# The last tile's rounding, transposes and bank copy shared between two engines, in an attention and ternary feed-forward kernel

## The chip, the cores and the metric

The kernel runs on one core of a Trainium2 chip. The metric is the device time of one execution in microseconds (us). The kernel before has a median of 99.2 us over 3 runs (99.07 to 100.43).

## The reference

`x` has 16 sequences of 56 tokens with 256 features (896 tokens in all). The layer is cross attention and then a feed-forward with ternary weights and activations quantised per token. Cut to what matters here:

```python
x = x + xattn(layernorm(x), ctx, Wq, Wkv_expand, Wout)       # 16 heads of 16, causal
def quant_weight(w): s = mean(|w|) + 1e-5; return clip(round(w / s), -1, 1), s
def quant_act(x):    s = max(|x|, axis=-1) / 127 + 1e-5; return clip(round(x / s), -128, 127), s
def qlinear(x, w):   return einsum(quantised x, quantised w) * xs * ws
h = silu(qlinear(y, w_gate)) * qlinear(y, w_up)               # y = layernorm(x); h: 896 x 1024
x = x + qlinear(h, w_down)                                    # 896 x 256
```

The change lies in the last step, for the last 128 tokens: `h` is multiplied by 1/s of its token, rounded, transposed and multiplied by `w_down`.

## The kernel before

The 896 tokens are 7 tiles of 128. Each engine has an instruction stream of its own, written as loops over slots `s`; semaphores order the engines. Slots 0 to 7 hold attention, slots 8 to 17 the feed-forward. Tile `t` is in gate and up products at slot `t + 8` (`GU0`), in the transposes of the gated values at slot `t + 10` (`HT0`), in the down product at slot `t + 11` (`DN0`). For the last tile, t = 6, these are slots 14, 16 and 17.

For one tile the tail of the feed-forward is this. VectorE (DVE) writes `h_sb` in two halves of 512 columns (L808), takes the row maxima (L815), the scale (L822), its reciprocal `r_tok` (L829) and `s_out` (L831). `round_h` (L302) then writes the rounded codes of a half into `h_int`, an alias of `wf_sb`, which is the name that the profile shows. `ROUNDER` gives the engine of each half: GpSimd (POOL) for tiles 0 to 5, DVE for both halves of tile 6. TensorE (PE) transposes eight 128x128 blocks as f16 into one PSUM bank (`transpose_gated`, L1100), ScalarE (ACT) copies the whole bank to `hT` (`read_misc`, kind `ht`, L552 in its helper), and PE multiplies the eight blocks of `hT` with `wdT` into a bank (`down_projection`, through the helper of L892). The end of a tile is `FINISHER`: tiles 0 to 4 are scaled by ACT (L620) and added to `x` by POOL (L519); tiles 5 and 6 are finished by one DVE instruction (`add_down_product`, L847). Both write `o_sb`, which the profile calls `k_wide`. SP waits for the tiles in order and issues one output DMA of 128 KB each (L394).

The four PSUM banks `bank0` to `bank3` are shared by all jobs: `misc_no` numbers the jobs, a job takes bank `n % 4`, and `take_bank` makes PE wait until the reader of job `n - 4` is done. At the end the order of jobs is `ht` 4, `dn` 3, `ht` 5, `dn` 4, `ht` 6, `dn` 5, `dn` 6. The order on the engines there is:

- PE: slot 16 is transposes of tile 6, then the down product of tile 5; slot 17 is the down product of tile 6.
- POOL: in a slot first the roundings of tile `s - 8`, then `add_residual` of tile `s - 11`. Slot 14 holds tile 6's roundings (none before) and the add of tile 3; slot 15 the add of tile 4.
- DVE: slot 14 holds tile 6's roundings; slot 16 the finish of tile 5, slot 17 the finish of tile 6.

Of the kernel before, what the change touches and what calls it, by code (L numbers as in the profile page):

```python
# [5 lines left out]
ALU = mybir.AluOpType  # L6
# [3 lines left out]
P = 128  # L10
# [9 lines left out]
HT0 = GU0 + 2  # L20
# [42 lines left out]
             (3, 'gpsimd'): [(1, 0, 1), (1, 1, 1)]}  # L63

ROUNDER = [('gpsimd', 'gpsimd'), ('gpsimd', 'gpsimd'), ('gpsimd', 'gpsimd'), ('gpsimd', 'gpsimd'), ('gpsimd', 'gpsimd'),
           ('gpsimd', 'gpsimd'), ('vector', 'vector')]

FINISHER = ['gpsimd', 'gpsimd', 'gpsimd', 'gpsimd', 'gpsimd', 'vector', 'vector']

# [1 line left out]
def xattn_ffn(nc, x, ctx_512, wq, wkv, wout, w_gate, w_up, w_down, out):  # L71
# [47 lines left out]
    for t in range(NT):  # L119
        misc[XQ_SLOTS[t]] += [("xqT", t)]  # L120

    misc_no = {job: n for n, job in enumerate(misc[-1])}
    for s in range(SLOTS):
        at_jobs = [("aT", s - 2)] if 0 <= s - 2 < NP - 1 else []
        tr_jobs = [("tr", s - 1, 0), ("tr", s - 1, 1)] if 0 <= s - 1 < NP else []
        op_jobs = [("op", OP_AT[s])] if s in OP_AT else []
        pv_jobs = [("pv", s - 1)] if 0 <= s - 1 < NP else []
        ht_jobs = [("ht", s - HT0)] if 0 <= s - HT0 < NT else []
        dn_jobs = [("dn", s - DN0)] if 0 <= s - DN0 < NT else []
        at_last = [("aT", NP - 1)] if s == NP else []  # L130
        for job in at_jobs + tr_jobs + misc[s] + op_jobs + pv_jobs + at_last + ht_jobs + dn_jobs:
            misc_no[job] = len(misc_no)
# [4 lines left out]
    with ExitStack() as ctx:  # L137
# [158 lines left out]
        def round_h(eng, ops, engine, t, c):  # L296
            if ROUNDER[t][c] != engine:
                return
            eng.wait_ge(r_ready, t + 1)
            if t >= 2:  # L300
                eng.wait_ge(misc_written, misc_no[("ht", t - 2)] + 1)
            ops.tensor_scalar(h_int[:, t % 2, c, :], h_sb[:, t % 3, GC * c:GC * c + GC], r_tok[:, 1, t:t + 1], CODED,  # L302
                              ALU.mult, ALU.add).then_inc(hint_ready[engine, c], 1)

# [27 lines left out]
        def read_misc(eng, copy, job):  # L332
            n = misc_no[job]
            kind, i = job[0], job[1]
            bank = MI[n % NB]
            eng.wait_ge(misc_written, n + 1)
            if kind == "wkvT":
                last = copy(wkvT[:, :], bank[:, :])
            elif kind == "ctxT":
                last = copy(ctxT[:, 0:KT], bank[:, 0:KT])  # L340
            elif kind == "k":
                (j0, j1), hfs = job[2:]
                width = 2 * S * (j1 - j0)
                last = copy(kT[:, i, hfs[0]:hfs[-1] + 1, 2 * S * j0:2 * S * j1],
                            bank[:, 0:len(hfs) * width].rearrange("p (i k) -> p i k", i=len(hfs)))
            elif kind in ("wqT", "woT"):
                last = copy((wqT if kind == "wqT" else woT)[:, :, :],
                            bank[:, :].rearrange("p (i o) -> p i o", i=HALVES))
            elif kind == "xT":
                last = copy(xnT[:, :, P * i:P * i + P], bank[:, 0:C].rearrange("p (i o) -> p i o", i=HALVES))  # L350
            elif kind == "q":
                p0, p1 = job[1:]
                last = copy(qT[:, :, 2 * p0:2 * p1, 0:S],
                            bank[:, 0:2 * CT * (p1 - p0) // 2].rearrange("p (i b q) -> p i b q", i=HALVES, q=S), scale=SCALE)
            elif kind == "v":
                eng.wait_ge(pads_ready, 1)
                for par in range(2):
                    last = copy(v_wide[:, VB * i:VB * i + VB, :, HV * par:HV * par + HD],
                                bank[:, :].rearrange("p (b h d) -> p b h d", b=VB, d=HD),
                                scale=parity_mask[:, par:par + 1])  # L360
            elif kind == "mean":
                last = copy(w_scale[:, i:i + 1], bank[:, 0:1], bias=EPS)
            elif kind == "tr":

                if i >= 2:
                    eng.wait_ge(misc_written, misc_no[("pv", i - 2)] + 1)
                n0 = 4 * 2 * S * job[2]
                last = copy(pT[:, i % 2, n0:n0 + 4 * 2 * S].rearrange("p (m b q) -> p m b q", m=4, b=2),
                            bank[:, :].rearrange("p (m b q) -> p m b q", m=4, b=2)[:, :, :, 0:S])
            elif kind == "aT":  # L370
                last = copy(attnT[:, :, 2 * S * i:2 * S * i + 2 * S].rearrange("p i (b q) -> p i b q", b=2),
                            bank[:, 0:C].rearrange("p (i b q) -> p i b q", i=HALVES, b=2)[:, :, :, 0:S])
            elif kind == "xqT":
                codes = bank[:, :].bitcast(F16)[:, 0:C].rearrange("p (i o) -> p i o", i=HALVES)
                last = copy(xqT[:, i, :, :], codes, scale=256.0, bias=-1536.0)
            elif kind == "ht":
                if i >= 2:
                    eng.wait_ge(misc_written, misc_no[("dn", i - 2)] + 1)
                last = copy(hT[:, i % 2, :, :], bank[:, :].bitcast(F16).rearrange("p (c q) -> p c q", c=NC8),
                            scale=256.0, bias=-1536.0)  # L380
            last.then_inc(misc_read[n % NB], 1)

        @block.sync
# [156 lines left out]
        def _(act):  # L540
# [68 lines left out]

            def read_gated(s):  # L610
                if 0 <= s - HT0 < NT:
                    read_misc(act, copy, ("ht", s - HT0))

            def scale_down_product(s):
                t = s - DN0
# [29 lines left out]
        def _(dve):  # L645
            def copy(dst, src, scale=None, bias=None):
                if bias is not None:
                    return nc.vector.tensor_scalar(dst, src, 1.0, bias, ALU.mult, ALU.add)
                if scale is not None:
                    return nc.vector.tensor_scalar(dst, src, scale, 1.0, ALU.mult, ALU.mult)  # L650
                return nc.vector.tensor_copy(dst, src)  # L651
# [182 lines left out]
            def round_gated(s, c):  # L834
                t = s - GU0
                if 0 <= t < NT:
                    round_h(dve, nc.vector, "vector", t, c)

            def add_down_product(s):
                t = s - DN0  # L840
                if 0 <= t < NT:
                    if FINISHER[t] != "vector":
                        return
                    n = misc_no[("dn", t)]
                    dve.wait_ge(misc_written, n + 1)
                    dve.wait_ge(dn_scale_ready, t + 1)
                    nc.vector.scalar_tensor_tensor(o_sb[:, t, :], MI[n % NB][:, 0:C], s_out[:, 2, t:t + 1],  # L847
                                                   x_sb[:, t, :], ALU.mult, ALU.add).then_inc(misc_read[n % NB], 1)
# [18 lines left out]
            for s in range(NT_SLOT0, SLOTS):  # L867
                if s == NT_SLOT0:
                    divide_by_sums(s - 2)
                token_maxima(s)  # L870
                add_attention(s)
                token_scales(s)
                second_stats(s)
                gate_up_scales(s)
                invert_token_scales(s)
                second_moments(s)
                read_misc_banks(s, 0, None)
                if s == NT_SLOT0:
                    divide_by_sums(s - 1)
                gate_times_up(s, 0)  # L880
                gate_times_up(s, 1)
                gated_maxima(s)
                gated_scales(s)
                invert_gated_scales(s)
                round_gated(s, 0)
                round_gated(s, 1)
                add_down_product(s)

        @block.tensor
        def _(pe):  # L890
# [200 lines left out]
            def transpose_gated(s):  # L1091
                t = s - HT0
                if 0 <= t < NT:
                    codes_out = take_bank(("ht", t))[:, :].bitcast(F16)
                    for h in range(NG):
                        pe.wait_ge(*rounded(t, h))
                        codes = h_int[:, t % 2, h, :].bitcast(F16)
                        for c in range(HC):
                            c0 = GC * h + P * c
                            last = nc.tensor.transpose(codes_out[:, c0:c0 + P], codes[:, 2 * P * c:2 * P * c + 2 * P:2],  # L1100
                                                       ident_h[:, :])
                    last.then_inc(misc_written, 1)

            def down_projection(s):
                t = s - DN0
                if 0 <= t < NT:
                    bank = take_bank(("dn", t))
                    if t == 0:
                        pe.wait_ge(wt_in[2], 16)
                    wait_read(pe, ("ht", t))  # L1110
                    for c in range(NC8):
                        last = mm(bank[:, 0:C], hT[:, t % 2, c, :], wdT[:, :, c, :],
                                  start=(c == 0), stop=(c == NC8 - 1))
                    last.then_inc(misc_written, 1)
# [45 lines left out]
```

## Time and profile before

| | us |
|---|---|
| median of 3 runs | 99.2 |
| lowest and highest | 99.07, 100.43 |
| the profiled execution: its time | 99.2 |
| the profiled execution: span of its instructions | 97.4 |
| PE busy in the span | 81.4 (84%) |
| DVE busy | 72.8 (75%) |
| ACT busy | 59.1 (61%) |
| POOL busy | 56.0 (58%) |

The span is the time from the first to the last event on the core; 1.8 us of the execution lie outside it. Starts in rows are in us from the start of the span. The busy shares are averages over stages of different nature, so what a change in one stage brings is read from the rows of that stage.

### The profile page before, as it was taken

What the parts mean: (1) busy time and instruction counts of PE and PEld (TensorE: products, weight loads), DVE (VectorE), ACT (ScalarE), POOL (GpSimd) and SP (SyncE); (2) the same over time, 40 slices, a digit from 0 to 9 for tenths busy, and PEclk for the clock granted to TensorE, in tenths of its full rate; (3) what the DMA queues carried; (4) which work ended last, traced back from release to release, by engine and by line L of the source; (5) the groups of instructions that cost most, each with busy time, mean ns of one, the idle gap of its engine ahead of it and who ended that gap; (6) DMA issues with size and microseconds to landing.
All of it is one profiled execution on the core that took longest, in us unless ns stands there. A gap on an engine that the chain in (4) does not pass through costs nothing.

```text
span 97.4 us, 2408 instructions
## 1 busy us (share of the span) xinstructions
PE 81.4 (84%) x872; PEld 56.7 (58%) x872; DVE 72.8 (75%) x180; ACT 59.1 (61%) x98; POOL 56.0 (58%) x108
## 2 busy tenths in 40 slices
PE   4997779769899859999999988799854989998470
PEld 1345556448559649786978756766322637756250
DVE  4662529789958991699948999375999999999721
ACT  0741413845097973759799799926728478987340
POOL 5650557199507999696948852525286174669400
PEclk9999999999999999999999999999999999999999
DMA  1999999000000000000293908100000000101322
GB/s 32 289 271 357 347 360 365 19 0 0 0 0 7 3 3 7 0 0 0 49 106 71 222 0 187 29 0 0 7 0 0 0 0 3 54 0 61 108 77 84
DMA packets 12579, 7.59 MB, mean 78 GB/s; under 512 B 7960, under 2 KB 12312, under 8 KB 12568
## 3 DMA queue, kind: packets, MB, share of 16 engines
q1 hardware_dynamic: 11292, 6.93, 26.3%
q10 hardware_dynamic: 1276, 0.51, 2.1%
q8 instruction: 7, 0.11, 0.5%
q14 instruction: 4, 0.03, 0.1%
HBM read 4.95 MB, written 0.92 MB: 60 GB/s over the span
## 4 chain that ended last, share of the span: by engine, by line
DVE 43%; PE 35%; issue 8%; DMA 5%; ACT 3%; ACTq 2%; POOL 1%; DVEq 0%; POOLq 0%
PE bank L892 20%; DVE amax L815 9%; DVE h_sb L808 7%; PE sc L892 6%; DMA ctx_sb<-in_ctx_dram 5%; DVE probs L719 4%; PE bank L1021 4%; DVE v_wide L650 3%; PE bank L1045 2%; DVE asum L703 2%; DVE mx L710 2%; DVE xnT L651 2%; DVE attn L734 2%; DVE s_tok L822 1%; DVE x_sb L750 1%
## 5 line engine op out<-in xcount | busy, mean ns | idle before, releaser
L289 POOL TENSOR_TENSOR k_wide<-kT,head_mask 128x896 f32<-128x896 f32 (+1 forms) x9 | 13.1, 1478 | 9.6 <-ACT kT L552 9.6
L892 PE MATMUL sc<-wT,xqT 128*128 128x512 bf16 x56 | 13.9, 380 | 3.4 <-DVE h_sb L808 3.4
L607 ACT ACTIVATE wf_sb<-sc,s_out 128x512 f32<-128x512 f32 x14 | 9.6, 688 | 7.5 <-PE sc L892 5.1
L302 POOL TENSOR_SCALAR wf_sb<-h_sb,r_tok 128x512 f32<-128x512 f32 x12 | 8.2, 692 | 9.5 <-DVE r_tok L829 9.5
L710 DVE TENSOR_REDUCE mx<-sc 128x16 f32<-128x896 f32 x8 | 8.7, 1088 | 3.6 <-PE sc L892 3.4
L808 DVE SCALAR_TENSOR_TENSOR h_sb<-sc,s_out,wf_sb 128x512 f32<-128x512 f32 x14 | 9.9, 740 | 1.1 <-ACT wf_sb L607 1.1
L892 PEld LDWEIGHTS sc<-wT,xqT 128*128 128x128 bf16 x56 | 5.0, 98 | 9.2 <-DVE h_sb L808 5.1
L562 ACT ACTIVATE probs<-probs 128x896 f32<-128x896 f32 x8 | 7.6, 952 | 4.2 <-DVE probs L719 3.8
L892 PEld LDWEIGHTS bank<-v_wide,pT 128*64 128x64 f32 x256 | 8.1, 138 | 2.3 <-issue 2.3
L892 PE MATMUL bank<-xnT,wqT 128*128 128x224 f32 (+1 forms) x40 | 7.4, 329 | 2.1 <-DVE xnT L651 1.5
L892 PE MATMUL bank<-v_wide,pT 128*64 128x34 f32 x256 | 9.0, 226 | 0.0
L552 ACT ACTIVATE hT<-bank 128x1024 bf16<-128x1024 f16 x7 | 7.2, 1023 | 3.0 <-PE bank L1100 2.3
L815 DVE TENSOR_REDUCE amax<-h_sb 128x1 f32<-128x1024 f32 x7 | 8.5, 1220 | 0.2
L719 DVE TENSOR_TENSOR probs<-sc,mx 128x896 f32<-128x896 f32 x8 | 8.7, 1083 | 0.1
L552 ACT ACTIVATE pT<-bank 128x448 f32<-128x448 f32 x16 | 7.8, 542 | 1.4 <-PE bank L1021 1.0
L1021 PE MATMUL bank<-ident,probs 128*128 128x128 f32 x64 | 8.4, 273 | 0.0
L892 PE MATMUL bank<-woT,attnT 128*128 128x256 f32 x28 | 7.6, 394 | 0.4 <-ACT attnT L552 0.4
L892 PEld LDWEIGHTS bank<-xnT,wqT 128*128 128x128 f32 x40 | 6.2, 190 | 2.9 <-issue 2.9
L892 PE MATMUL bank<-wdT,hT 128*128 128x256 bf16 x56 | 7.3, 272 | 0.3 <-ACT hT L552 0.3
L892 PE MATMUL sc<-k_wide,qT 64*64 64x224 f32 x128 | 7.4, 349 | 0.0
L1021 PEld LDWEIGHTS bank<-ident,probs 128*128 128x128 f32 x64 | 7.2, 141 | 0.3 <-ACT probs L562 0.3
L892 PE MATMUL sc<-tern 128*128 128x512 bf16 x14 | 5.8, 574 | 1.3 <-DVE tern L654 1.3
(107 smaller groups left out, 166.9 us busy)
## 6 DMA issues: line engine op xcount, KB each, us to landing
wf_sb<-in_L_ffn_w_gate_dram SPq DMA_DIRECT2D x1, 1024.0 KB, 8.6
wf_sb<-in_L_ffn_w_up_dram SPq DMA_DIRECT2D x1, 1024.0 KB, 11.0
wf_sb<-in_L_ffn_w_down_dram SPq DMA_DIRECT2D x1, 1024.0 KB, 12.3
out_dram<-k_wide SPq DMA_DIRECT2D x7, 128.0 KB, 1.7
x_sb<-in_x_dram SPq DMA_DIRECT2D x2, 256.0 KB, 4.4
x_sb<-in_x_dram SPq DMA_DIRECT2D x1, 384.0 KB, 6.1
wq_sb<-in_L_xattn_Wq_dram ACTq DMA_DIRECT2D x1, 256.0 KB, 4.6
wo_sb<-in_L_xattn_Wout_dram SPq DMA_DIRECT2D x1, 256.0 KB, 8.9
```

The costliest lines, as they stand in the source:

```text
L289: ops.tensor_tensor(k_wide[:, c, hf, :, cols], kT[:, c, hf, None, cols].to_broadcast([P, RH, n]), head_mask[:, 0:RH, None].to_broadcast([P ...
L302: ops.tensor_scalar(h_int[:, t % 2, c, :], h_sb[:, t % 3, GC * c:GC * c + GC], r_tok[:, 1, t:t + 1], CODED, ALU.mult, ALU.add).then_inc(hi ...
L552: return nc.scalar.activation(dst, src, ACT.Copy, scale=scale, bias=bias)
L562: nc.scalar.activation(probs[:, u % R, :, 0:S], probs[:, u % R, :, 0:S], ACT.Exp).then_inc(exp_ready, 1)
L607: nc.scalar.activation(g_sb[:, t % 2, GC * c:GC * c + GC], SC[:, j % 4, :], ACT.Silu, scale=s_out[:, 0, t:t + 1]).then_inc(silu_ready, 1)
L650: return nc.vector.tensor_scalar(dst, src, scale, 1.0, ALU.mult, ALU.mult)
L710: nc.vector.tensor_reduce(mx[:, u % R, :].rearrange("p (r h) -> p r h", r=2), scores_of(u), axis=AX_X, op=ALU.max).then_inc(max_ready, 1)
L719: nc.vector.tensor_tensor(probs[:, u % R, :, 0:S].rearrange("p (r h) k -> p r h k", r=2), scores_of(u), mx[:, u % R, :].rearrange("p (r h) ...
L808: nc.vector.scalar_tensor_tensor(h_sb[:, t % 3, cols], SC[:, j % 4, :], s_out[:, 1, t:t + 1], g_sb[:, t % 2, cols], ALU.mult, ALU.mult).th ...
L815: nc.vector.tensor_reduce(amax[:, 1, t:t + 1], h_sb[:, t % 3, :], axis=AX_X, op=ALU.max, apply_absolute_value=True).then_inc(h_amax_ready, 1)
L892: return nc.tensor.matmul(*a, **k)
L1021: last = nc.tensor.transpose(bank[:, P * m:P * m + P], probs[:, u % R, h0:h0 + 2, :].rearrange("p h k -> p (h k)"), ident[:, :])
```

## The change

The second half of tile 6 is rounded by POOL in place of DVE. The job `("ht", 6)` becomes two jobs `("ht", 6, 0)` and `("ht", 6, 1)` with a bank each; the transposes of each half raise `misc_written` on their own. ACT copies the first bank (512 columns), DVE the second (`read_last_gated`, placed ahead of `add_down_product` in DVE's slot). The down product of tile 6 waits for the first copy before its first block and for the second before its fifth. Tiles 0 to 5 are computed as before, with a job name of three fields. The diff without two lines that only rename:

```diff
-           ('gpsimd', 'gpsimd'), ('vector', 'vector')]
+           ('gpsimd', 'gpsimd'), ('vector', 'gpsimd')]
+    def ht_halves(t):
+        return [("ht", t, 0), ("ht", t, 1)] if t == NT - 1 else [("ht", t, None)]
-        ht_jobs = [("ht", s - HT0)] if 0 <= s - HT0 < NT else []
+        ht_jobs = ht_halves(s - HT0) if 0 <= s - HT0 < NT else []
...
             elif kind == "ht":
                 if i >= 2:
                     eng.wait_ge(misc_written, misc_no[("dn", i - 2)] + 1)
-                last = copy(hT[:, i % 2, :, :], bank[:, :].bitcast(F16).rearrange("p (c q) -> p c q", c=NC8),
-                            scale=256.0, bias=-1536.0)
+                c0, c1 = (0, NC8) if job[2] is None else (HC * job[2], HC * job[2] + HC)
+                codes = bank[:, :].bitcast(F16)[:, 0:P * (c1 - c0)]
+                last = copy(hT[:, i % 2, c0:c1, :], codes.rearrange("p (c q) -> p c q", q=P), scale=256.0, bias=-1536.0)
...
-                    read_misc(act, copy, ("ht", s - HT0))
+                    read_misc(act, copy, ht_halves(s - HT0)[0])
...
-                    return nc.vector.tensor_scalar(dst, src, 1.0, bias, ALU.mult, ALU.add)
+                    return nc.vector.tensor_scalar(dst, src, 1.0 if scale is None else scale, bias, ALU.mult, ALU.add)
...
+            def read_last_gated(s):
+                if s - HT0 == NT - 1:
+                    read_misc(dve, copy, ("ht", NT - 1, 1))
...
                 round_gated(s, 1)
+                read_last_gated(s)
                 add_down_product(s)
...
-                    codes_out = take_bank(("ht", t))[:, :].bitcast(F16)
+                    jobs = ht_halves(t)
                     for h in range(NG):
+                        if h < len(jobs):
+                            codes_out = take_bank(jobs[h])[:, :].bitcast(F16)
                         pe.wait_ge(*rounded(t, h))
                         codes = h_int[:, t % 2, h, :].bitcast(F16)
                         for c in range(HC):
-                            c0 = GC * h + P * c
+                            c0 = P * c + (GC * h if len(jobs) == 1 else 0)
                             last = nc.tensor.transpose(codes_out[:, c0:c0 + P], codes[:, 2 * P * c:2 * P * c + 2 * P:2],
                                                        ident_h[:, :])
-                    last.then_inc(misc_written, 1)
+                        if h >= NG - len(jobs):
+                            last.then_inc(misc_written, 1)
...
-                    wait_read(pe, ("ht", t))
                     for c in range(NC8):
+                        if c % HC == 0 and c // HC < len(ht_halves(t)):
+                            wait_read(pe, ht_halves(t)[c // HC])
                         last = mm(bank[:, 0:C], hT[:, t % 2, c, :], wdT[:, :, c, :],
                                   start=(c == 0), stop=(c == NC8 - 1))
```

## Rows read from the trace of the kernel before

**Rows 1.** Chain of waits, its last part: start us, us, what

```profile
92.11 0.41 PE bank L1100 x4
92.54 1.03 ACT hT L552
93.71 1.05 PE bank L892 x8
94.78 0.48 DVE k_wide L847
```

**Rows 2.** Timeline: start us, us, engine line op out<-in xcount [idle before <-releaser]

```profile
90.48 0.16 DVE L829 RECIPROCAL r_tok<-s_tok 128x1 f32<-128x1 f32 x1
90.68 0.49 DVE L302 TENSOR_SCALAR wf_sb<-h_sb,r_tok 128x512 f32<-128x512 f32 x1
91.04 0.72 POOL L519 TENSOR_TENSOR k_wide<-k_wide,x_sb 128x256 f32<-128x256 f32 x1 [0.58 <-ACT k_wide L620]
...
91.08 0.97 DVE L302 TENSOR_SCALAR wf_sb<-h_sb,r_tok 128x512 f32<-128x512 f32 x1
```

**Rows 3.** Timeline of PE's weight loads, DVE and ACT behind the roundings

```profile
91.28 0.24 PEld L1100 LDWEIGHTS bank<-ident_h,wf_sb 128*128 128x128 f16 x4 [1.15 <-issue]
...
92.10 0.23 PEld L1100 LDWEIGHTS bank<-ident_h,wf_sb 128*128 128x128 f16 x4 [0.58 <-DVE wf_sb L302]
...
92.29 0.81 PEld L892 LDWEIGHTS bank<-wdT,hT 128*128 128x128 bf16 x8
...
93.42 0.48 DVE L847 SCALAR_TENSOR_TENSOR k_wide<-bank,s_out,x_sb 128x256 f32<-128x256 f32 x1 [1.37 <-PE bank L892]
93.68 0.78 PEld L892 LDWEIGHTS bank<-wdT,hT 128*128 128x128 bf16 x8 [0.58 <-issue]
```

**Rows 4.** Timeline of DVE and POOL where they multiply by the head mask

```profile
10.58 0.62 DVE L289 TENSOR_TENSOR k_wide<-kT,head_mask 128x448 f32<-128x448 f32 x1 [1.33 <-ACT kT L552]
10.62 1.38 POOL L289 TENSOR_TENSOR k_wide<-kT,head_mask 128x448 f32<-128x448 f32 x1 [4.17 <-ACT kT L552]
...
16.16 0.93 POOL L289 TENSOR_TENSOR k_wide<-kT,head_mask 128x448 f32<-128x448 f32 x1
```

**Rows 5.** Timeline of tile 5's reciprocal and its roundings on POOL

```profile
87.46 0.16 DVE L829 RECIPROCAL r_tok<-s_tok 128x1 f32<-128x1 f32 x1
...
87.72 0.69 POOL L302 TENSOR_SCALAR wf_sb<-h_sb,r_tok 128x512 f32<-128x512 f32 x1 [0.96 <-DVE r_tok L829]
...
89.05 1.41 POOL L519 TENSOR_TENSOR k_wide<-k_wide,x_sb 128x256 f32<-128x256 f32 x2
```

**Rows 6.** Groups of instructions by line: forms xcount | busy us, mean ns

```profile
L552 ACT ACTIVATE hT<-bank 128x1024 bf16<-128x1024 f16 x7 | 7.2, 1023 | 3.0 <-PE bank L1100 2.3
...
L650 DVE TENSOR_SCALAR v_wide<-bank,parity_mask 128x512 f32<-128x512 f32 x4 | 2.8, 745 | 0.4 <-PE bank L892 0.4
...
L552 ACT ACTIVATE wkvT<-bank 128x512 f32<-128x512 f32 x1 | 0.6, 597 | 1.3 <-PE bank L929 1.3
```

**Rows 7.** Timeline of SP: two early loads, the outputs of tiles 2 and 3, 3, and 6

```profile
2.24 0.92 SPq L311 DMA_DIRECT2D x_sb<-in_x_dram  x2
...
89.80 1.34 SPq L394 DMA_DIRECT2D out_dram<-k_wide  x2
...
90.48 0.66 SPq L394 DMA_DIRECT2D out_dram<-k_wide  x1
...
95.29 0.33 SPq L394 DMA_DIRECT2D out_dram<-k_wide  x1
```

**Rows 8.** Stretches: A:B us, PE, PEld, DVE, ACT, POOL busy (x), PEclk, DMA share, GB/s

```profile
90.70:90.90 0.20, 0.00 (x0) 0.00 (x0) 0.20 (x2) 0.20 (x1) 0.00 (x0) 1.00 0.98 317
...
91.70:91.90 0.20, 0.00 (x0) 0.00 (x0) 0.20 (x1) 0.00 (x0) 0.07 (x1) 1.00 1.03 353
...
96.10:96.30 0.20, 0.00 (x0) 0.00 (x0) 0.00 (x0) 0.00 (x0) 0.00 (x0) 1.00 0.77 266
```

**Rows 9.** DMA issues: KB each, median us from issue to landing

```profile
out_dram<-k_wide SPq DMA_DIRECT2D x7, 128.0 KB, 1.7
```

More of the change, by code:

```diff
@@ L300, in round_h @@
             if t >= 2:
-                eng.wait_ge(misc_written, misc_no[("ht", t - 2)] + 1)
+                eng.wait_ge(misc_written, misc_no[("ht", t - 2, None)] + 1)
             ops.tensor_scalar(h_int[:, t % 2, c, :], h_sb[:, t % 3, GC * c:GC * c + GC], r_tok[:, 1, t:t + 1], CODED,
```

## The prediction

> **What bounds the kernel now.** I read the chain of waits first, and only its end, since everything the change touches lies behind the last tile's scale. The chain ends as DVE rounding, four transposes on PE, the ACT copy of the bank, the eight matmuls of the down product, DVE's finish [rows 1]. Then come the issue of the last output DMA at 95.29, its landing after about 1.7 us, and the last 0.4 us to the end of the span at 97.4 [rows 7, 9]. So the path is serial, and a saving in it moves the end by as much, unless the output DMAs get in the way.
>
> The timeline then says how long each piece is. DVE rounds the two halves one after the other: the first from 90.68 to 91.17, the second from 91.08 to 92.05 [rows 2]. The same instruction on the same shape takes 0.49 the first time and 0.97 the second. Between them POOL began its add of tile 4, at 91.04, 0.04 before DVE's second rounding, and it ended at 91.76 [rows 2]. DVE's end at 92.05 is 0.29 behind POOL's end. My reading is that the two instructions cannot run together and that the later one stood still for 0.97 - 0.49 = 0.48 us. The trace has a second such pair with the roles exchanged: DVE's multiply by the head mask starts at 10.58, POOL's at 10.62; DVE takes 0.62 and POOL 1.38, where the same form takes POOL 0.93 alone [rows 4]. Again the one that began 0.04 later paid, 0.45 us, and it ended 12.00 - 11.20 = 0.80 us behind the other's end, which is 0.13 less than a whole instruction.
>
> Last, the PE rows. Weight loads show the pace of PE's stream best. Behind the second half's transposes the down product of tile 5 starts 0.19 later (92.10 to 92.29) and its eight loads end at 93.10. Tile 6's down product starts loading at 93.68 [rows 3]. The 0.58 us between is the wait for the ACT copy, 92.54 to 93.56 [rows 1], plus 0.12 from its end to PE's load. These two, the second rounding and this gap, are all that the change can shorten.
>
> **The change part by part.** *Rounding.* DVE's first half stays where it is, 90.68 to 91.17. POOL's half waits for the same `r_tok`. In tile 5 POOL's rounding started 0.26 after the start of `r_tok` (87.46 to 87.72) [rows 5]; from 90.48 this gives 90.74, and 0.69 alone would end it at 91.43. But DVE starts 0.06 earlier, and by the two pairs the later one waits. With the 0.13 of start-up that POOL had done in its pair, it ends 0.69 - 0.13 = 0.56 behind 91.17, at 91.73. Against 92.05 that is 0.32 us earlier. The bounds are 91.43 (no conflict, 0.62 earlier) and 91.86 (its whole 0.69 behind DVE's end at 91.17, 0.19 earlier). I take 91.73, as the only pair in which POOL lost shows it.
>
> The Trainium skill has the rule: SBUF — State Buffer, section "SBUF: two separate sides", says that DVE and GpSimd share a port pair that goes whole to the instruction that starts first, while the other blocks. The two pairs here agree, in both orders [rows 2, 4]. Perfetto Trace Analysis, section "Optimizing Scalar/DVE Operations", warns that moving work between these two engines might therefore not help; the full form of that warning, both roundings strictly in series, is the 91.86 above, so by it the saving would be 0.13 smaller. What the warning leaves out is that the series already exists before the change, with a longer add in the middle.
>
> *POOL's queue.* POOL's rounding now stands in slot 14 ahead of the add of tile 3 (queued at 89.05 with tile 2's, two adds in 1.41 [rows 5]) and of tile 4 (91.04). POOL waits with both behind it until 90.74. The adds then run at about 0.70 each: tile 3 to 92.43, tile 4 to 93.13. Who waits for them is SP alone, for the output DMAs. They no longer lie in front of any rounding.
>
> *Transposes and down product of tile 5.* PE's second group waits for POOL: 91.73 plus 0.06 (92.05 to 92.10 before) is 91.79. The down product of tile 5 loads from 91.79 + 0.19 = 91.98, and its loads end at 92.79. The bank numbers move by one: the four last jobs now take the banks of `ht` 4, `dn` 3, `ht` 5 and `dn` 4. The last of their readers is ACT's scaling of `dn` 4, and it ended before POOL could start tile 4's add at 91.04 [rows 2], so PE waits for no bank.
>
> *The copy.* ACT's half takes 0.60 in place of 1.02: the 512-column row, against the 1024-column one [rows 6]. The copy began 0.44 behind the start of the transposes before it (92.10 to 92.54) [rows 1, 3]. The first half's start at 91.28, so ACT copies from 91.72 to 92.32. DVE's half has no row of its own kind (f16 in PSUM to bf16). The nearest is the f32 copy with a scale, 0.745 for 512 columns [rows 6]; the lower bound is 0.49, its quick rounding of as many columns [rows 2]. I take the slow one: it starts at 91.79 + 0.44 = 92.23 and ends at 92.98. PE needs ACT's half at 92.79 and has it 0.47 earlier. It needs DVE's half for the fifth block at 92.79 + 0.40 = 93.19, and 92.98 plus 0.05 to 0.12 is in time by about 0.1. So the gap of 0.58 closes entirely, and its cover is thin for DVE's half only: a copy of 0.95 would cost 0.1 to 0.2.
>
> *DVE's queue.* The copy stands ahead of tile 5's finish. That finish waits for PE until 93.42 - 0.31 = 93.11 [rows 3], so the copy ending at 92.98 delays nothing.
>
> *Sum.* Tile 6's down product loads from 92.79 in place of 93.68: 0.31 by the rounding and 0.58 by the gap, 0.89 together. DVE's finish starts at 94.78 - 0.89 = 93.89, the DMA issue moves from 95.29 to 94.40. Span 97.4 - 0.9 = 96.5; the profiled execution took 99.2, the same as the median, so 99.2 - 0.9 = 98.3 us.
>
> *The output DMAs.* Tile 3's was issued at 90.48 and tile 6's at 95.29, 0.03 behind DVE's finish (94.78 + 0.48) [rows 1, 7]. Now the four come at 92.46, 93.16, 93.62 (93.11 + 0.48 + 0.03) and 94.40, four in 1.94 us in place of 4.81. An issue takes 0.33, but tile 3's, 0.68 behind tile 2's, took 0.66 [rows 7]. At the 266 to 353 GB/s of the transfers' stretches 128 KB need 0.4 to 0.5 us [rows 8], less than the distances between the issues (0.46 to 0.78). Against a slow issue stand the early loads, two issues in 0.92 us [rows 7]. I cost this at nothing and keep 0.3 as an upper bound for a late last transfer.
>
> **The rivals.** *R1, the outputs queue up, and the end comes later than before.* Full data rate came at 90.7 for tile 2 and at 91.7 for tile 3, 1.0 apart, although the issues were 0.68 apart [rows 8]. If 1.0 us is the least distance of two such transfers, tile 3's starts at 92.46 + 0.9 = 93.36 and tile 6's at 96.36, against about 96.15 before [rows 8]: 0.2 later, 99.4 us. It decides from a distance of 0.93 us on. Against it: two early loads were issued in 0.92 together [rows 7], and the one pair shows an excess of only 0.3.
>
> *R2, part of that.* Each close issue costs 0.33 more, and the last one inherits 0.3: 98.6 us.
>
> *R3, POOL comes first.* If POOL's rounding starts before DVE's, DVE ends at 91.43 + 0.29 = 91.72 and POOL at 91.43. PE transposes both halves from 91.77 in one go, and tile 5's down product loads from 92.20 and tile 6's from 93.01: 0.67 gained, 98.5 us. For it: a lead of only 0.06. Against it: POOL's start behind `r_tok` was 0.26, DVE's is 0.20 [rows 2, 5].
>
> *R4, no conflict.* Both roundings free, 91.43: tile 5's down product from 91.72, tile 6's from 92.53, 1.15 gained, 98.05 us. Against it stand both pairs [rows 2, 4].
>
> *R5, no change that shows.* PE waits in the middle of the accumulation for DVE's copy or for the queue of semaphores, or the execution's start moves: 98.9 to 99.3. Only the gap's 0.58 or less would be at stake, as the roundings alone give 0.3.
>
> **How the numbers follow.** The forecast of 98.3 (with the bound of 91.86, 98.4) has 0.55, R1 0.07, R2 0.13, R3 0.08, R4 0.09, R5 0.08. The likeliest case's own range is 98.1 to 98.5. From 97.9 to 98.9 lie the forecast, R2, R3 and R4, 0.85 in all; since other runs of the kernel before spread from 99.07 up I set 97.9 to 99.0. Faster or slower by over 2% (2.0 us, about what a measurement of this kernel tells from no change) needs a time below 97.2 or above 101.2. No case reaches either; I leave 0.03 and 0.02.
>
> **What would show it.** In the profile after: one DVE rounding of about 0.49 at 90.7 and one POOL rounding that takes about 1.0 in place of 0.69 (R4: 0.69; R3: DVE's takes 1.0). The two down products' loads back to back, no idle before the last eight. ACT's last copy 0.60, DVE's 0.5 to 0.75. POOL's two adds behind 91.7. The last DMA issued at about 94.4 with 1.7 us to landing (R1: over 3; R2: about 2.1). It would be wrong if the conflict costs more than one instruction, if the fifth matmul waits, or if the last output waits behind the others.

## The result, and the profile after

The changed kernel has a median of 98.45 us over 9 runs beside 99.2 us of the kernel before. The ratio to the kernel before is 0.9931 (95% interval 0.9902 to 0.9959). Two more comparisons gave 0.9922 (0.9894 to 0.9951) and 0.9946 (0.9917 to 0.9974). In the three comparisons it is faster by 0.5 to 0.8%, some 0.5 to 0.8 us: each interval lies below 1, though the difference is under 2%. The prediction was 98.3 us, 97.9 to 99.0.

Some executions, of the kernel before too, are granted half of TensorE's clock for a stretch in the first 30 us and end 2 to 9 us later: the medians here are over all executions and the ratios over the others alone, the time of a single execution with such a stretch is not compared, and in every profile used below the clock is full in the last 15 us, where the change lies. The start of the last tile's reciprocal also varies by itself, from 90.07 to 91.16 us between the profiles whose span is under 98 us. So I measure the **tail**: from the start of the last reciprocal (`r_tok`) to the start of DVE's last finish (`k_wide<-bank,s_out,x_sb`). It agrees to 0.01 us between the three profiles of the changed kernel (3.55, 3.55, 3.56) and between the two of the version in which ACT rounds (3.23, 3.23); the other versions have one profile each.

The end of the chain of waits in a profile of the changed kernel (the one with the span of 96.4 us); start us, us, what:

```profile
90.22 0.17 DVE r_tok L834
90.40 0.09 issue
90.49 0.99 POOL wf_sb L306
91.48 0.14 issue
91.61 0.38 PE bank L1112 x4
92.00 1.76 PE bank L902 x16
93.76 0.03 issue
93.78 0.48 DVE k_wide L856
```

The ACT copy of [rows 1] is gone from the chain, and the last sixteen matmuls are one piece. The tail is 93.78 - 90.22 = 3.56 us; before it is 94.78 - 90.48 = 4.30 [rows 1, 2]. That is 0.74 less. The same kernel's timeline shows the pieces; they answer [rows 2, 3, 5]:

```profile
90.42 0.49 DVE L306 TENSOR_SCALAR wf_sb<-h_sb,r_tok 128x512 f32<-128x512 f32 x1
90.49 0.98 POOL L306 TENSOR_SCALAR wf_sb<-h_sb,r_tok 128x512 f32<-128x512 f32 x1 [0.96 <-DVE r_tok L834]
91.03 0.24 PEld L1112 LDWEIGHTS bank<-ident_h,wf_sb 128*128 128x128 f16 x4 [1.15 <-issue]
...
91.48 0.60 ACT L557 ACTIVATE hT<-bank 128x512 bf16<-128x512 f16 x1 [0.77 <-PE bank L1112]
91.58 0.24 PEld L1112 LDWEIGHTS bank<-ident_h,wf_sb 128*128 128x128 f16 x4 [0.32 <-issue]
...
91.78 1.68 PEld L902 LDWEIGHTS bank<-wdT,hT 128*128 128x128 bf16 x16
91.83 1.91 PE L902 MATMUL bank<-wdT,hT 128*128 128x256 bf16 x16
...
92.03 0.43 DVE L653 TENSOR_SCALAR hT<-bank 128x512 bf16<-128x512 f16 x1 [1.12 <-PE bank L1112]
...
92.91 0.48 DVE L856 SCALAR_TENSOR_TENSOR k_wide<-bank,s_out,x_sb 128x256 f32<-128x256 f32 x1 [0.45 <-PE bank L902]
93.78 0.48 DVE L856 SCALAR_TENSOR_TENSOR k_wide<-bank,s_out,x_sb 128x256 f32<-128x256 f32 x1 [0.39 <-PE bank L902]
```

POOL's rounding takes 0.98 in place of its usual 0.69, and ends 0.56 behind DVE's. Sixteen weight loads run in one row of 1.68 with no idle before the last eight, where there were 0.58 us [rows 3]. From the end of the last finish (94.26) to the end of the span it is 2.1 us, as before (95.26 to 97.4).

The output DMAs did not pile up. The stretches of the same profile (columns as in [rows 8]) show one transfer's full rate at 93.1, 93.7, 94.3 and 95.1, and the four issues before them took 0.33 each (the last four rows: start us, us, issue on SP):

```profile
93.10:93.30 0.20, 0.20 (x4) 0.18 (x3) 0.20 (x1) 0.00 (x0) 0.00 (x0) 1.00 1.03 353
...
93.70:93.90 0.20, 0.04 (x1) 0.00 (x0) 0.12 (x1) 0.00 (x0) 0.00 (x0) 1.00 0.91 312
...
94.30:94.50 0.20, 0.00 (x0) 0.00 (x0) 0.00 (x0) 0.00 (x0) 0.00 (x0) 1.00 0.98 338
...
95.10:95.30 0.20, 0.00 (x0) 0.00 (x0) 0.00 (x0) 0.00 (x0) 0.00 (x0) 1.00 0.73 251
...
92.19 0.33 SPq L399 DMA_DIRECT2D out_dram<-k_wide  x1
...
92.87 0.33 SPq L399 DMA_DIRECT2D out_dram<-k_wide  x1
...
93.42 0.33 SPq L399 DMA_DIRECT2D out_dram<-k_wide  x1
...
94.30 0.33 SPq L399 DMA_DIRECT2D out_dram<-k_wide  x1
```

### The profile page after: what moved, and what is told of

Read it like the earlier page. It is cut to its first block, busy times and chain, and to the rows that moved or that the text cites. A ratio compares the mean times of both kernels' runs of the same rounds, so it can differ in the third digit from the quotient of the medians.

```text
span 99.1 us, 2411 instructions
## 1 busy us (share of the span) xinstructions
PE 81.9 (83%) x872; PEld 57.4 (58%) x872; DVE 72.4 (73%) x180; ACT 58.6 (59%) x98; POOL 56.9 (57%) x109
## 4 chain that ended last, share of the span: by engine, by line
DVE 41%; PE 37%; issue 7%; DMA 6%; POOL 2%; ACTq 2%; ACT 1%; POOLq 0%; DVEq 0%
PE bank L902 21%; DVE amax L820 9%; DVE h_sb L813 7%; PE sc L902 7%; DMA ctx_sb<-in_ctx_dram 6%; DVE probs L724 4%; PE bank L1031 4%; DVE v_wide L655 3%; PE bank L1055 2%; DVE asum L708 2%; DVE mx L715 2%; DVE xnT L656 2%; DVE attn L739 2%; DVE s_tok L827 1%; DVE x_sb L755 1%
## 5 line engine op out<-in xcount | busy, mean ns | idle before, releaser
L306 POOL TENSOR_SCALAR wf_sb<-h_sb,r_tok 128x512 f32<-128x512 f32 x13 | 9.1, 714 | 10.5 <-DVE r_tok L834 10.5
L557 ACT ACTIVATE hT<-bank 128x1024 bf16<-128x1024 f16 (+1 forms) x7 | 6.7, 962 | 2.2 <-PE bank L1112 1.4
```

The lines of the kernel that those rows point to most:

```text
L557: return nc.scalar.activation(dst, src, ACT.Copy, scale=scale, bias=bias)
```

## The experiments

**The change once more.** The kernel as changed.

> The changed kernel as it is. The tail is read from the start of the last tile's reciprocal (L834 here) to the start of DVE's last finish: 4.30 us in the kernel before (90.48 to 94.78), 3.55 in the changed kernel's first profile. My theory (0.3 from the rounding, 0.6 from the closed gap, a few hundredths lost to PE): 3.5 to 3.6 again, and a median 0.7 to 0.9 us under the kernel before. The rival that the output DMAs pile up: more than 2.1 us from the last DMA's issue to the end of the span, which was 2.1 before.

Measured: 98.52 us against 99.36, ratio 0.9922. The tail is 3.55 us (91.16 to 94.71), and 2.1 us follow the end of the last finish. Its span, 97.3, is that of the kernel before, because this execution reached the reciprocal 0.68 later: a span alone cannot show a change of this size.

**The rounding alone.**

```diff
-           ('gpsimd', 'gpsimd'), ('vector', 'vector')]
+           ('gpsimd', 'gpsimd'), ('vector', 'gpsimd')]
```

> The kernel before with one edit: POOL rounds the last tile's second half. One bank, one copy by ACT. My theory: the two roundings stand in series, POOL's ends 1.24 behind the start of the reciprocal in place of 1.57, so the tail is 4.30 - 0.32 = 3.98, the gap of 0.58 stays, median 0.3 under before. Rival, that moving work to POOL brings nothing because the two engines exclude each other: tail 4.30, median as before.

Measured: 99.02 us against 99.36, ratio 0.9947 (0.9912 to 0.9983). The timeline of DVE, POOL and PE's loads:

```profile
90.16 0.16 DVE L829 RECIPROCAL r_tok<-s_tok 128x1 f32<-128x1 f32 x1
...
90.42 0.98 POOL L302 TENSOR_SCALAR wf_sb<-h_sb,r_tok 128x512 f32<-128x512 f32 x1 [0.96 <-DVE r_tok L829]
...
91.45 0.23 PEld L1100 LDWEIGHTS bank<-ident_h,wf_sb 128*128 128x128 f16 x4 [0.25 <-POOL wf_sb L302]
...
93.03 0.78 PEld L892 LDWEIGHTS bank<-wdT,hT 128*128 128x128 bf16 x8 [0.58 <-issue]
...
94.13 0.48 DVE L847 SCALAR_TENSOR_TENSOR k_wide<-bank,s_out,x_sb 128x256 f32<-128x256 f32 x1 [0.88 <-PE bank L892]
```

The tail is 94.13 - 90.16 = 3.97 (3.98 expected), and the gap of 0.58 is still there. Moving work to POOL brings 0.33 although the two engines exclude each other, so the rival falls.

**The split alone.** The changed kernel with `ROUNDER[6]` back to `('vector', 'vector')`.

> The changed kernel with both halves rounded by DVE as before: two banks and two copies alone. My theory: the second rounding again takes 0.97 beside POOL's add of tile 4, and the gap of 0.58 between the two down products closes to nothing: tail 4.30 - 0.55 = 3.75, median 0.5 to 0.6 under before. Rival, that the split is worth nothing without the earlier rounding: 4.30.

Measured: 98.78 us against 99.36, ratio 0.9952 (0.9926 to 0.9977). The timeline:

```profile
90.43 0.16 DVE L834 RECIPROCAL r_tok<-s_tok 128x1 f32<-128x1 f32 x1
...
92.11 0.24 PEld L1112 LDWEIGHTS bank<-ident_h,wf_sb 128*128 128x128 f16 x4 [0.65 <-issue]
...
92.31 1.68 PEld L902 LDWEIGHTS bank<-wdT,hT 128*128 128x128 bf16 x16
...
94.31 0.48 DVE L856 SCALAR_TENSOR_TENSOR k_wide<-bank,s_out,x_sb 128x256 f32<-128x256 f32 x1 [0.39 <-PE bank L902]
```

The tail is 94.31 - 90.43 = 3.88, not 3.75. The gap is closed, the sixteen loads are one row of 1.68; but of the 0.55 expected from it 0.13 is missing. Two places hold it, and both are in the changed kernel too:

- PE's load for the second transposes starts 1.68 behind the reciprocal (92.11 - 90.43), 1.62 before (92.10 - 90.48), behind the same pair of roundings. Behind POOL's rounding PE starts after 0.05 with one bank (91.40 to 91.45 in the experiment above) and after 0.11 with two (91.47 to 91.58). So the second bank costs 0.06 there. The rows point to the added wait on the bank's reader just in front (`take_bank`): in the kernel before, the first group, which stands behind such a wait, starts 0.11 behind the end of DVE's rounding (91.17 to 91.28) and the second, which does not, 0.05 (92.05 to 92.10) [rows 2, 3]. It was not tested by itself.
- The two down products are 0.87 apart (DVE's finishes, 93.44 and 94.31), not the 0.81 that eight weight loads take.

**The split, with DVE's roundings undisturbed.**

```diff
-           ('gpsimd', 'gpsimd'), ('vector', 'gpsimd')]
+           ('gpsimd', 'gpsimd'), ('vector', 'vector')]
...
                     wait_read(pool, ("dn", t))
+                    if t == 4:
+                        pool.wait_ge(*rounded(NT - 1, 1))
```

> As the split alone, and POOL's add of tile 4 waits until DVE has rounded the last half, so that nothing stands beside DVE's two roundings. My theory of the exclusion: both take 0.49, they overlap by 0.09, and the second ends 0.20 + 0.40 + 0.49 = 1.09 behind the start of the reciprocal (1.24 in the changed kernel, 1.57 before): tail 3.55 - 0.15 = 3.40, median 0.1 to 0.2 under the changed kernel. Rival, that DVE's second rounding is slow for a reason of its own (the first was 0.49, the second 0.97, back to back): it takes 0.97 again and the tail is 3.75 as with the split alone.

Measured: 98.29 us against 99.36, ratio 0.9885 (0.9849 to 0.9921). The timeline:

```profile
90.23 0.16 DVE L836 RECIPROCAL r_tok<-s_tok 128x1 f32<-128x1 f32 x1
...
90.43 0.88 DVE L306 TENSOR_SCALAR wf_sb<-h_sb,r_tok 128x512 f32<-128x512 f32 x2
...
91.42 0.24 PEld L1114 LDWEIGHTS bank<-ident_h,wf_sb 128*128 128x128 f16 x4 [0.16 <-issue]
91.45 0.73 POOL L526 TENSOR_TENSOR k_wide<-k_wide,x_sb 128x256 f32<-128x256 f32 x1 [1.25 <-DVE wf_sb L306]
```

DVE's two roundings take 0.88 together, 1.37 before with POOL's add between. So the second one's 0.97 of [rows 2] was the add and nothing of its own. The tail is 93.63 - 90.23 = 3.40, as expected to the hundredth. With no work moved to POOL at all, this is 0.15 shorter than the change.

**The same wait in the kernel before.** One bank, one copy, both halves on DVE, and only the two added lines above.

> The kernel before with one edit: POOL's add of tile 4 waits for DVE's last rounding; one bank, one copy, both halves rounded by DVE. Theory of the exclusion: the second rounding takes 0.49 in place of 0.97, the tail is 4.30 - 0.48 = 3.82. Rival: the last output DMAs or the later add of tile 4 give it back, span less than 0.2 shorter behind the reciprocal.

Measured, one execution (102.11 us, not compared); the timeline:

```profile
93.86 0.16 DVE L831 RECIPROCAL r_tok<-s_tok 128x1 f32<-128x1 f32 x1
...
94.06 0.88 DVE L302 TENSOR_SCALAR wf_sb<-h_sb,r_tok 128x512 f32<-128x512 f32 x2
...
97.68 0.48 DVE L849 SCALAR_TENSOR_TENSOR k_wide<-bank,s_out,x_sb 128x256 f32<-128x256 f32 x1 [0.88 <-PE bank L894]
```

The roundings take 0.88, the tail is 97.68 - 93.86 = 3.82, and from the last finish's end (98.16) to the end of the span (100.3) it is 2.1. One wait on an engine with time to spare is worth 0.48 of the 0.74 that the whole change brings, by the tail of this one profile; no median was taken of this version.

**One reader.** ACT copies both banks, DVE none.

```diff
-                    read_misc(act, copy, ht_halves(s - HT0)[0])
+                    for job in ht_halves(s - HT0):
+                        read_misc(act, copy, job)
...
-                read_last_gated(s)
                 add_down_product(s)
```

> The changed kernel, but ACT copies both banks of the last tile, one after the other, and DVE none. My theory (the halves let the copy run under tile 5's down product; who copies does not matter): ACT's copies run from 1.25 to 1.85 and to about 2.42 behind the start of the reciprocal, PE needs the second at about 2.8, so the tail from the reciprocal to DVE's last finish stays at 3.55 and the median is that of the changed kernel. Rival, that the second engine is what closes the gap: PE's last eight loads wait again, tail 3.7 or more.

Measured: 98.65 us against 99.19, ratio 0.9912 (0.9871 to 0.9953). The timeline:

```profile
98.55 0.16 DVE L835 RECIPROCAL r_tok<-s_tok 128x1 f32<-128x1 f32 x1
...
99.81 1.15 ACT L557 ACTIVATE hT<-bank 128x512 bf16<-128x512 f16 x2 [0.77 <-PE bank L1112]
...
100.11 1.68 PEld L902 LDWEIGHTS bank<-wdT,hT 128*128 128x128 bf16 x16
...
102.11 0.48 DVE L857 SCALAR_TENSOR_TENSOR k_wide<-bank,s_out,x_sb 128x256 f32<-128x256 f32 x1 [0.39 <-PE bank L902]
```

The tail is 3.56, that of the change. ACT's second copy ends 2.41 behind the reciprocal, and PE wants it at 1.56 + 0.87 + 0.4 = 2.8. So two banks with a wait for each close the gap; the second engine adds nothing here. Whether two copies out of one bank would do as well was not tried.

**ACT rounds the second half.** In slot 15, between ACT's copy of tile 5 and its scaling of tile 4:

```diff
-           ('gpsimd', 'gpsimd'), ('vector', 'gpsimd')]
+           ('gpsimd', 'gpsimd'), ('vector', 'scalar')]
...
                 read_gated(s)
+                if s == HT0 + NT - 2:
+                    act.wait_ge(r_ready, NT)
+                    act.wait_ge(misc_written, misc_no[("ht", NT - 3, None)] + 1)
+                    nc.scalar.activation(h_int[:, (NT - 1) % 2, 1, :], h_sb[:, (NT - 1) % 3, GC:2 * GC], ACT.Copy,
+                                         scale=r_tok[:, 1, NT - 1:NT], bias=CODED).then_inc(hint_ready["scalar", 1], 1)
                 scale_down_product(s)
```

> The changed kernel, but ACT rounds the second half in POOL's place, ahead of its scaling of tile 4's down product, and POOL's adds go on as before. My theory of the exclusion between DVE and POOL: DVE's half takes 0.49 and ACT's 0.6 to 0.7, both at once, so the second half is ready 0.83 to 0.95 behind the start of the reciprocal (1.24 in the changed kernel); PE's second group follows the first without a pause, the tail is 3.25 in place of 3.55, median 0.3 under the changed kernel. Rival, that any two engines slow each other on this tile: DVE or ACT takes near 1.0 and the tail is 3.5.

Measured: 98.33 us against 99.19, ratio 0.9881 (0.9826 to 0.9935). The timeline:

```profile
98.06 0.16 DVE L839 RECIPROCAL r_tok<-s_tok 128x1 f32<-128x1 f32 x1
...
98.26 0.48 DVE L306 TENSOR_SCALAR wf_sb<-h_sb,r_tok 128x512 f32<-128x512 f32 x1
...
98.26 0.72 ACT L650 ACTIVATE wf_sb<-h_sb,r_tok 128x512 f32<-128x512 f32 x1
...
98.86 0.47 PEld L1117 LDWEIGHTS bank<-ident_h,wf_sb 128*128 128x128 f16 x8 [1.15 <-issue]
...
101.29 0.48 DVE L861 SCALAR_TENSOR_TENSOR k_wide<-bank,s_out,x_sb 128x256 f32<-128x256 f32 x1 [0.39 <-PE bank L907]
```

DVE and ACT work at once on the same tile, and DVE keeps its 0.48; ACT takes 0.72, a little over the 0.6 to 0.7 expected. So it is not so that any two engines slow each other on this tile: DVE's and POOL's roundings do, DVE's and ACT's do not. PE's eight transposes need no pause, and the tail is 3.23 (3.25 expected). This is the shortest tail of all.

**Both once more, on one chip.**

> The changed kernel once more, for a comparison on one chip with the version in which ACT rounds the second half: tail 3.55, median 0.7 to 0.8 under the kernel before.

> The version in which ACT rounds the second half, once more: tail 3.23, median 1.0 to 1.1 under the kernel before and 0.3 under the changed kernel.

Measured: 98.54 us for the change, ratio 0.9946 (0.9917 to 0.9974), tail 3.56; 97.97 us for ACT's rounding, ratio 0.9899 (0.985 to 0.9948), tail 3.23; 99.19 for the kernel before. The medians are 0.57 apart, the tails 0.33. The tails came as expected, the medians did not: 0.65 under the kernel before where 0.7 to 0.8 was expected, and 1.22 where 1.0 to 1.1 was. The tail in the profiles is the sharper measure, and the intervals of the two ratios overlap.

**The halves exchanged.** `ROUNDER[6] = ('gpsimd', 'vector')`.

> The changed kernel with the halves exchanged: POOL rounds the first, DVE the second. Theory (the one that starts 0.06 later waits): DVE again takes 0.49 and POOL 0.98; the half that PE wants first is then the late one, PE transposes eight blocks in one go from 1.3 behind the reciprocal, tail 3.75 against 3.55. Rival, that the order of the halves does not matter: 3.55.

Measured, one execution (106.4 us, not compared); the timeline:

```profile
98.38 0.49 DVE L306 TENSOR_SCALAR wf_sb<-h_sb,r_tok 128x512 f32<-128x512 f32 x1
98.45 0.98 POOL L306 TENSOR_SCALAR wf_sb<-h_sb,r_tok 128x512 f32<-128x512 f32 x1 [0.96 <-DVE r_tok L834]
...
99.97 1.68 PEld L902 LDWEIGHTS bank<-wdT,hT 128*128 128x128 bf16 x16
100.00 0.60 ACT L557 ACTIVATE hT<-bank 128x512 bf16<-128x512 f16 x1 [1.32 <-PE bank L1112]
```

DVE is first again by 0.07 and POOL pays again. PE waits for POOL with everything, and the tail is 101.97 - 98.19 = 3.78 (3.75 expected). So the engine that comes late must have the half that PE wants last. The gap stays closed here, although PE transposed both halves in one go: the sixteen loads are again one row. ACT's copy of the first half starts 0.03 behind the first of them (100.00 - 99.97), where the whole copy of the kernel before starts 0.25 behind (92.54 - 92.29); how much the earlier start and how much the shorter copy closes, no run separates.

**DVE's copy behind its finish of tile 5.**

```diff
-                read_last_gated(s)
                 add_down_product(s)
+                read_last_gated(s)
```

> The changed kernel with DVE's copy of the second bank placed behind its finish of tile 5. Theory: that finish waits for tile 5's down product until 2.68 behind the reciprocal, the copy runs from 3.14 to 3.56, the fifth block of the last product waits for it until about 3.62 in place of 2.8, and the tail is 3.55 + 0.8 = 4.4, longer than the 4.30 of the kernel before. Rival, that PE's stream hides a late second half: 3.6 to 3.8.

Measured, one execution (105.84 us, not compared); the timeline:

```profile
97.28 0.17 DVE L834 RECIPROCAL r_tok<-s_tok 128x1 f32<-128x1 f32 x1
...
99.97 0.48 DVE L856 SCALAR_TENSOR_TENSOR k_wide<-bank,s_out,x_sb 128x256 f32<-128x256 f32 x1 [2.00 <-PE bank L902]
100.37 0.41 DVE L653 TENSOR_SCALAR hT<-bank 128x512 bf16<-128x512 f16 x1
...
100.84 0.33 PEld L902 LDWEIGHTS bank<-wdT,hT 128*128 128x128 bf16 x4 [0.75 <-DVE hT L653]
```

PE waits 0.75 for DVE before the last four loads, and the tail is 101.49 - 97.28 = 4.21, 0.65 longer than the change and nearly that of the kernel before. I expected 4.4. The stall is nearly the 0.8 expected, but the copy started 0.05 earlier (3.09 behind the reciprocal), and of the stall 0.1 does not reach the end: behind it PE's last four loads take 0.33, where four of the sixteen in a row of 1.68 take 0.42, and DVE's finish starts 0.32 behind them as ever, 100.84 + 0.33 + 0.32 = 101.49. The placing of one line in DVE's slot is worth most of what the change brings.

**Tile 3's add ahead of POOL's rounding.** In the last tile's slot `add_residual(s)` comes before `round_gated`.

> The changed kernel, but POOL's add of tile 3 stands ahead of its rounding of the last tile, so that tile 3's output DMA goes out 1.8 us earlier and only three output DMAs follow each other closely. Theory: the DMAs are not on the path; tail from the reciprocal to DVE's last finish 3.55, and 2.1 us from the end of that finish to the end of the span, both as in the changed kernel. Rival R2 (close issues delay the last one): the end of the span comes closer by 0.1 to 0.3.

Measured, one execution: 98.05 us, tail 93.63 - 90.07 = 3.56, and 2.1 us from the last finish (94.11) to the end of the span (96.2). Taking one DMA out of the close row changes nothing.

The tails together, in us:

| kernel | rounding of the halves | banks, readers | tail |
|---|---|---|---|
| before | DVE, DVE beside POOL's add | 1, ACT | 4.30 |
| rounding alone | DVE, POOL | 1, ACT | 3.97 |
| split alone | DVE, DVE beside POOL's add | 2, ACT and DVE | 3.88 |
| hold alone | DVE, DVE | 1, ACT | 3.82 |
| **the change** | DVE, POOL | 2, ACT and DVE | 3.55, 3.56 |
| one reader | DVE, POOL | 2, ACT | 3.56 |
| split and hold | DVE, DVE | 2, ACT and DVE | 3.40 |
| ACT rounds | DVE, ACT | 2, ACT and DVE | 3.23, 3.23 |
| halves exchanged | POOL, DVE | 2, ACT and DVE | 3.78 |
| copy behind the finish | DVE, POOL | 2, ACT and late DVE | 4.21 |
| tile 3's add first | DVE, POOL | 2, ACT and DVE | 3.56 |

The two parts add up: 0.33 by the rounding and 0.42 by the split are the 0.75 of the change.

## Why the prediction was right, point by point

The measured 98.45 us alone does not tell the forecast from R2 (98.6) or R3 (98.5), and the range of 97.9 to 99.0 holds executions of the kernel before too (down to 98.6). What bears the forecast out are the rows: each step that it named came, and together they are worth 0.74 to 0.75 us where it had 0.89.

**The exclusion of DVE and POOL** was read rightly. POOL's rounding ended 1.25 us behind the reciprocal's start (91.47 - 90.22), as worked out (91.73 - 90.48), 0.56 behind DVE's end. Holding back POOL's add and rounding on ACT showed the same from the other side. The rule of the Trainium skill, SBUF — State Buffer, section "SBUF: two separate sides", is that whichever of the two starts first has the shared port pair, for DVE instructions in a two-port mode or with two inputs in SBUF. The trace agrees: of DVE's 0.49 and POOL's 0.98 the one that started 0.07 later is the long one. But POOL's rounding did not end its whole 0.69 behind DVE's end: it ended 0.56 behind, 0.13 less, as in the pair of another instruction from which the forecast had taken the 0.13. That it would be the same for this instruction rested on one pair; it came again in every profile of this rounding. The warning of the Trainium skill, Perfetto Trace Analysis, section "Optimizing Scalar/DVE Operations", that moving work between the two might not help did not decide here: the rounding alone brought 0.33. ACT is the better place, by another 0.32 to 0.33.

The exclusion does not hold for whatever the two engines do, and the forecast left that limit out. In the kernel before POOL's twelve roundings of tiles 0 to 5 take 0.69 each, though DVE writes `h_sb` beside them; tile 5's first POOL rounding of [rows 5] runs from 87.72 to 88.41 beside this row:

```profile
87.60 1.40 DVE L808 SCALAR_TENSOR_TENSOR h_sb<-sc,s_out,wf_sb 128x512 f32<-128x512 f32 x2
```

DVE is not slowed either: its fourteen writes of `h_sb` take 0.73 to 0.75 each, with POOL's roundings beside them (70.93) or without (67.56). DVE's row maxima take 1.22 and its copy of the second bank 0.43 with POOL's adds beside them, and the adds keep their 0.72 to 0.73. The DVE instructions that collided are the rounding and the multiply by the head mask, whose pair of 0.62 to 0.63 and 1.38 comes again in each of the 14 profiles. Which property of them decides was not separated by a run.

**The gap between the down products** closed as forecast, but the sum was sized too large. The forecast took 0.31 and 0.58, 0.89 in all, and 0.74 to 0.75 was measured. The missing 0.15 stand in PE's part of the tail. The forecast's tail is 1.25 + 0.06 + 0.19 + 0.81 + 1.10 = 3.41, the measured one 1.25 + 0.11 + 0.20 + 0.87 + 1.13 = 3.56: POOL's end, PE's step to the second transposes, from there to tile 5's down product, the pace of one down product, and from the first load of the last one to DVE's finish. The 1.10 was read from the kernel before (93.68 to 94.78), where PE had paused ahead of the last product; behind tile 5's product it is 1.13 in both kernels (92.29 to 93.42 and 91.78 to 92.91). The largest term, 0.06, is the pace: the forecast held that weight loads show it best, and eight loads take 0.81, but the finishes are 0.87 apart. The loads run ahead of the matmuls: sixteen matmuls take 1.91 and eight take 1.04 (92.34 to 93.38 in the kernel before), so eight more cost 0.87.

**The copies.** ACT's took 0.60 as taken from its row. DVE's took 0.43, not 0.745, and less than the lower bound of 0.49. It was covered either way, so the sum did not feel it. That the second copy needs no second engine was not seen in the forecast, though its numbers held it: ACT was free at 92.32 there and PE wanted the half at 93.19.

**The order in DVE's queue** was rightly named as harmless; the experiment with the copy behind the finish puts the price of the other order at 0.65.

**The output DMAs** are not on the path. R1 and R2 fall: full rates came 0.6 apart in the profile after, and 0.8 before the last, where 0.93 would have been needed for R1, each issue took 0.33, and the end stayed 2.1 to 2.2 us behind the last finish in every profile. Why tile 3's issue took 0.66 in the kernel before and its data came late [rows 7, 8] stays open.

**The other rivals.** R3 (POOL first) did not happen in any profile: DVE's lead of 0.06 to 0.07 held each time. R4 (no conflict) did not happen between DVE and POOL. ACT's rounding shows what it would have brought: a tail of 3.23, 1.07 under before, where 1.15 were worked out; of the missing 0.08 the pace is 0.06 again. R5 falls with the tail, 0.74 shorter, and with the sixteen loads in one row.

## What to carry to other kernels

When the same instruction on the same shape takes twice as long the second time, look at what another engine began just before it: here a residual add of POOL that only an output DMA waited for held up DVE's rounding on the critical path by 0.48 us, and one wait that holds the add back gives two thirds of what the whole rewrite takes off the tail. If a half of the work is to go to another engine, give it to one that does not slow the first (here ACT, not POOL), and give the late engine the half that is wanted last. Splitting a copy pays because the product can begin on half of the data, copied in 0.60 us where the whole takes 1.02, and the second half's copy is covered by the products running meanwhile, not because two engines copy.

## What the runs showed of the hardware

- DVE copies 512 columns of f16 from PSUM to bf16 with a scale and an offset in 0.41 to 0.43 us, where the f32 form with a scale takes 0.745 [rows 6]; ACT takes 0.60 for the same f16 half. In the Trainium skill, VectorE: DVE Perf Modes, section "The perf-mode tier table (the rule you actually need)" gives such operations at most twice the base rate where an operand is in PSUM. These rows are within that, but they do not test it: the two forms differ in the type and in the scalar operand at once.
- ACT rounds 512 columns of f32 from SBUF in 0.72 us, DVE in 0.49, POOL in 0.69.
- DVE's rounding that starts 0.04 behind POOL's add takes 0.97 in place of 0.49 and ends 0.29 behind the add [rows 2]; POOL's rounding that starts 0.06 to 0.07 behind DVE's takes 0.98 in place of 0.69 and ends 0.56 behind it. In every such pair of these profiles the one that began first kept its usual time.
